# Order of the first loads and of the weight splitting in a two-layer attention kernel

## What is computed

```python
x = x + layer0(x, bias0, mask0, null_kv, ...)
x = x + layer1(x, mask1, null_kv, ...)
```

## Time and profile before

| | us |
|---|---|
| median of 3 runs | 2144.53 |
| lowest and highest | 2143.86, 2146.55 |
| the profiled execution, as timed | 2146.16 |
| its span in the profile | 2144.4 |
| TensorE busy | 2084.0 (97%) |
| VectorE, ScalarE, GpSimd busy | 1601.1, 1555.1, 1027.0 |

### The profile page before, as it was taken

The page is one execution under the profiler, slowest core; times in us unless marked ns, Lnnn a source line. Parts: engine busy times, 40 slices in busy tenths (PEclk is TensorE's granted clock), DMA queues, the critical chain, the costliest instruction groups (busy, mean ns, idle before and its releaser), DMA issues.

```text
span 2144.4 us, 72068 instructions
## 1 busy us (share of the span) xinstructions
PE 2084.0 (97%) x26363; PEld 1860.3 (87%) x26363; DVE 1601.1 (75%) x3422; ACT 1555.1 (73%) x6241; POOL 1027.0 (48%) x1510
## 2 busy tenths in 40 slices
PE   5899999999999999999999999999999999999987
PEld 4788988988988988988988988988988988988876
DVE  5877777777777777777777777777777777777765
ACT  3767777777777777777777777777777777777775
POOL 3445444445544444544544544544544544544543
PEclk8999999999999999999999999999999999999998
DMA  7212222222222212222222222222222212222211
GB/s 233 83 55 73 63 72 62 61 60 69 66 71 60 66 59 66 70 65 61 70 58 61 75 63 63 70 57 62 75 63 63 70 57 62 75 63 63 68 52 42
DMA packets 183034, 147.47 MB, mean 69 GB/s; under 512 B 121440, under 2 KB 125616, under 8 KB 182992
## 3 DMA queue, kind: packets, MB, share of 16 engines
q1 hardware_dynamic: 179008, 141.31, 22.3%
q10 hardware_dynamic: 3296, 4.46, 0.7%
q0 software_dynamic: 688, 1.14, 0.3%
HBM read 98.56 MB, written 37.77 MB: 64 GB/s over the span
## 4 chain that ended last, share of the span: by engine, by line
PE 92%; ACT 2%; SPq 2%; DVE 2%; issue 1%; POOL 1%; DMA 0%; POOLq 0%; DVEq 0%; ACTq 0%
PE psum L709 33%; PE psum L615 18%; PE psum L581 16%; PE psum L692 8%; PE psum L674 8%; PE psum L543 3%; PE psum L632 3%; PE psum L592 2%; SPq L386 1%; ACT o_hi L907 1%; ACT probs L901 1%; POOL probs L1479 0%; DMA xa<-in_x_dram 0%; DVE wo_lo L1188 0%; PE psum L623 0%
## 5 line engine op out<-in xcount | busy, mean ns | idle before, releaser
L901 ACT ACTIVATE probs<-probs,neg_max 128x129 f32<-128x129 f32 (+3 forms) x2048 | 712.3, 351 | 56.4 <-DVE neg_max L1144 56.3
L1469 POOL TENSOR_TENSOR masked_bias<-bias,pad_neg 128x516 f32<-128x516 f32 (+3 forms) x512 | 396.2, 806 | 211.8 <-DVE probs L1138 206.1
L1479 POOL TENSOR_TENSOR probs<-probs,den_inv 128x512 f32<-128x512 f32 (+3 forms) x512 | 369.4, 743 | 149.4 <-DVE den_inv L1149 149.4
L1491 POOL TENSOR_TENSOR y_out<-y_out,res 128x512 f32<-128x512 f32 x128 | 165.9, 1296 | 527.0 <-ACT y_out L865 527.0
L901 ACT ACTIVATION_READ_ACCUMULATOR probs<-probs,neg_max 128x1 f32 x2048 | 385.4, 188 | 0.0
L1154 DVE STREAM_TRANSPOSE probs_t<-probs 128x512 f32<-128x512 f32 (+3 forms) x512 | 229.9, 487 | 196.0 <-POOL probs L1479 194.9
L1138 DVE TENSOR_TENSOR probs<-psum,masked_bias 128x648 f32<-128x648 f32 x256 | 212.7, 831 | 114.3 <-PE psum L674 110.1
L709 PE MATMUL psum<-wo_hi,o_hi 128*128 128x512 f32 x1024 | 273.2, 409 | 8.2 <-ACT o_hi L907 7.5
L907 ACT ACTIVATE o_hi<-psum,null_v_col 128x512 fp32r<-128x512 f32 x256 | 162.1, 684 | 156.0 <-PE psum L692 156.0
L709 PE MATMUL psum<-wo_hi,o_lo 128*128 128x512 f32 x1024 | 262.5, 398 | 0.0
L709 PE MATMUL psum<-wo_lo,o_hi 128*128 128x512 f32 x1024 | 261.3, 397 | 0.0
(11 more groups left out here) (133 smaller groups left out, 3915.5 us busy)
## 6 DMA issues: line engine op xcount, KB each, us to landing
res<-in_x_dram SPq DMA_DIRECT2D x64, 256.0 KB, 2.7
v_rep<-v_kept SPq DMA_DIRECT2D x512, 32.0 KB, 1.8
x_of<-y_out SPq DMA_DIRECT2D x64, 256.0 KB, 2.1
res<-x_of SPq DMA_DIRECT2D x64, 256.0 KB, 2.7
out_dram<-y_out SPq DMA_DIRECT2D x64, 256.0 KB, 2.1
xa<-in_x_dram SPq DMA_DIRECT2D x63, 256.0 KB, 2.7
xa<-x_of SPq DMA_DIRECT2D x63, 256.0 KB, 2.7
q_aside<-qp SPq DMA_DIRECT2D x32, 256.0 KB, 3.1
```

The costliest lines, as they stand in the source:

```text
L901: x_ = nc.scalar.activation(s, s, ACT.Exp, bias=neg_max[:, b, n:n + 1], accum_out=den[:, b, n:n + 1])
L1469: m = nc.gpsimd.tensor_tensor(block(masked_bias, b), block(bias[u.layer], b), pad_neg[u.layer][:, 0:WIDTH[b]].unsqueeze(1).to_broadcast([P ...
L1479: m = nc.gpsimd.tensor_tensor(some, some, den_inv[:, b, :].unsqueeze(2).to_broadcast([P, 4, n]), ALU.mult)
```

## The change

- SyncE asks for the third input ahead of the bias loads, and for only 8 of the 16 bias loads; these have a semaphore of their own.
- GpSimd's queue asks for the other 8, behind w1, w2 and b2. GpSimd waits for both halves.
- ScalarE asks for weight pieces 4 to 7 after the first query halves are copied (before: ahead of the position network's first steps), and for 8 to 11 after the second halves, at the end of `begin`; the four high parts of pieces 4 to 7 all come behind that. `second0` gets one high part more, `first0` one fewer.
- Of the low parts of pieces 4 to 11, VectorE makes none in `begin` (before: one), four in `first0` (before: five) and four in `second0` (before: two). The statistics of the fourth input move from the start of `first0` to ahead of the first bias addition, and its normalising comes ahead of two of the row maxima.

```diff
--- before.py
+++ after.py
@@ -338,8 +338,9 @@
         sp_passed, dve_passed, pool_passed, pe_passed, act_passed = (
             sem(n) for n in ("sp_passed", "dve_passed", "pool_passed", "pe_passed", "act_passed"))
 
-        null_loaded, gain_loaded, null_row_loaded, null_v_loaded, g_out_loaded, rest_loaded, w1_loaded = (
-            sem(n) for n in ("null_loaded", "gain_loaded", "null_row_loaded", "null_v_loaded", "g_out_loaded", "rest_loaded", "w1_loaded"))
+        null_loaded, gain_loaded, null_row_loaded, null_v_loaded, g_out_loaded, w1_loaded = (
+            sem(n) for n in ("null_loaded", "gain_loaded", "null_row_loaded", "null_v_loaded", "g_out_loaded", "w1_loaded"))
+        rest_loaded = [sem(f"rest_loaded{n}") for n in range(2)]
         rows_loaded = [sem(f"rows_loaded{n}") for n in range(2)]
         raw_loaded = [sem(f"raw_loaded{n}") for n in range(4 * KC)]
         hi_done, lo_done = sem("hi_done"), sem("lo_done")
@@ -490,11 +491,10 @@
                 sp.dma_start(y_out[:, :], x[1]).then_inc(y_loaded, 16)
                 load_pieces(sp, range(KC))
                 start(sp, rows_loads[:3], rows_loaded[0])
-                start(sp, rest_loads[:8], rest_loaded)
+                load_xa(n)
+                start(sp, rest_loads[:8], rest_loaded[0])
                 for k in range(2):
                     sp.dma_start(keep[k][:, :], row((keep0, keep1)[k][0], S)).then_inc(keep_loaded[k], 16)
-                load_xa(n)
-                start(sp, rest_loads[8:], rest_loaded)
                 start(sp, rows_loads[3:], rows_loaded[1])
                 start(sp, [(null_v[:, :], row(null_kv[1], DH))], null_v_loaded)
                 load_res(w.even)
@@ -956,18 +956,17 @@
                 split_x(w.odd)
                 act.wait_ge(gain_loaded, 16 * len(gain_loads))
                 high_parts(range(KC))
-                load_pieces(act, range(KC, 2 * KC))
                 rstd_of_h(0)
                 sigmoid(0)
                 for k in range(2):
                     take_half(w, 0, k)
-                load_pieces(act, range(2 * KC, 3 * KC))
+                load_pieces(act, range(KC, 2 * KC))
                 null_norm()
-                high_parts((KC, KC + 1))
                 rstd_of_input(n)
                 for k in range(2):
                     take_half(w, 1, k)
-                high_parts((KC + 2, KC + 3))
+                load_pieces(act, range(2 * KC, 3 * KC))
+                high_parts(range(KC, 2 * KC))
 
             def first0(u, v, w, n, then):
                 rstd_of_input(w.odd)
@@ -980,14 +979,14 @@
                 take_half(w, 0, 0)
                 high_parts((2 * KC,))
                 take_half(w, 0, 1)
-                high_parts((2 * KC + 1, 2 * KC + 2))
+                high_parts((2 * KC + 1,))
                 act.wait_ge(null_loaded, 16 * len(null_loads))
                 split_o(u)
 
             def second0(u, v, w, n, then):
                 exponential(u, 0)
                 exponential(u, 1)
-                high_parts((2 * KC + 3,))
+                high_parts((2 * KC + 2, 2 * KC + 3))
                 copy_biases()
                 act.wait_ge(xn_done, w.odd.xdone)
                 take_y(v)
@@ -1283,36 +1282,34 @@
                 null_key_scaled()
                 input_statistics(n)
                 normalise(n)
-                low_parts((KC,))
                 second_layer()
                 dve.wait_ge(null_v_loaded, 16)
                 take_pair_v(w)
+                input_statistics(n2)
                 add_bias(then, 0)
 
             def first0(u, v, w, n, then):
-                input_statistics(w.odd)
                 add_bias(u, 1)
                 row_max(u, 3)
                 split_x(w.even)
+                normalise(w.odd)
                 row_max(u, 1)
-                normalise(w.odd)
                 row_max(u, 2)
                 row_max(u, 0)
                 normed(1)
                 inverse_sum(u, 0)
                 split_x(w.odd)
-                low_parts((KC + 1,))
+                low_parts((KC,))
                 turn(u, 0)
                 silu(1)
                 inverse_sum(u, 1)
+                low_parts((KC + 1,))
+                silu_transposed(1)
                 low_parts((KC + 2,))
-                silu_transposed(1)
-                low_parts((KC + 3,))
                 turn(u, 1)
                 last_layer()
-                low_parts((2 * KC,))
+                low_parts((KC + 3,))
                 diagonals_transposed()
-                low_parts((2 * KC + 1,))
                 add_bias(then, 0)
 
             def second0(u, v, w, n, then):
@@ -1325,11 +1322,12 @@
                 split_o(v, 1)
                 inverse_sum(u, 0)
                 dve.wait_ge(g_out_loaded, 16 * len(g_out_loads))
-                low_parts((2 * KC + 2,))
+                low_parts((2 * KC, 2 * KC + 1))
                 turn(u, 0)
                 centre_output(v)
                 inverse_sum(u, 1)
                 take_kvt(w)
+                low_parts((2 * KC + 2,))
                 turn(u, 1)
                 take_pair_v(w)
                 input_statistics(n)
@@ -1458,6 +1456,7 @@
 
             pool.wait_ge(raw_loaded[KC - 1], 32)
             start(pool, w1_loads, w1_loaded)
+            start(pool, rest_loads[8:], rest_loaded[1])
 
             def mask_bias(u):
                 wait(pool, keep_loaded[u.layer], u.sdone * 16)
@@ -1491,7 +1490,8 @@
                 nc.gpsimd.tensor_tensor(y_out[:, :], y_out[:, :], res[:, :], ALU.add).then_inc(out_done, 1)
 
             def begin(w, n, n2, then):
-                pool.wait_ge(rest_loaded, 16 * len(rest_loads))
+                for n_loaded in range(2):
+                    pool.wait_ge(rest_loaded[n_loaded], 16 * 8)
                 for b in range(BLOCKS):
                     square = block(bias[0], b)[:, :, 1 + b * R:]
                     nc.gpsimd.tensor_tensor(square, square, later[:, :].unsqueeze(1).to_broadcast([P, 4, R]),
```

## The result

The changed kernel takes 2165.86 us (median of 4 runs, 2164.94 to 2166.6) against 2145.54 before (2143.86 to 2147.49): a ratio of 1.0091, 95% interval 1.0079 to 1.0103. It is 20 us slower. The forecast was 2141.3 us with a range to 2146.5, so both the size and the side are wrong.

A forecast was written before the change was run, and what follows sets the result against it. TensorE bounds the kernel from 107.73 us on, so early gains shift the end one for one. The first addition 4.0 us sooner and 0.8 lost behind it make -3.2: 2144.5 - 3.2 = 2141.3 us, range 2136.4 to 2146.5.

The forecast's parts named there:

- GpSimd's half: Eight bias loads on GpSimd's queue behind w1, w2 and b2; forecast to land last, at 38.7 us.
- B: Moment the last bias load is there for GpSimd: 38.7 us forecast, 42.71 before; 26.65 + 2L for longer L.
- L: Landing time of GpSimd's loads beside ScalarE's weights: 5.8 us taken for w2, 6.3 for the last bias load.
- M: Start of VectorE's first addition of the masked bias: 44.3 us forecast, 4.0 sooner than 48.33.
- The copy of the keys: SyncE's request for this copy, forecast near 28 us instead of 42.08, costed at nothing.
- M minus B: From the last bias load's arrival to VectorE's first addition: 5.6 us, left as it is by the change.
- VectorE's floor for M: VectorE's readiness for the first addition after position product and fourth input's statistics: 40.8 us, the limit if bias comes sooner.
- From M to the steady part: First addition through `first0` and `second0`: 0.8 us lost together, bounds -0.6 and +2.
- The 0.8 won: Ahead of the second unit's additions, a VectorE low part of 1.40 us is gone: 0.8 us won, bounds 0 to 1.4.
- The third: Rival: GpSimd's loads starved behind ScalarE's weights; B 48.7, 2151.2 us at L = 11; chance 0.09.
- The second: Rival: the transfers on the shared engines were the limit; B stays at 42.7, 2145.3 us; chance 0.13.
- The chance of 0.08 for slower: Probability given to the whole kernel becoming slower by over 0.2%.

The follow-up runs named there:

- e6: The kernel before with only the bias loads cut into 32 of 32 partitions x 2 heads, all on SyncE's queue: 2143.01 us, ratio 0.9983.
- e8: The changed kernel with bias loads cut into 32 of 32 partitions x 2 heads, still split over both queues, and 2048 bytes of descriptor space: 2138.62 us.
- e9: e8 with the order of high and low parts in the first two units as before the change: 2137.39 us, ratio 0.9958.
- e10: e8 with only ScalarE's one high part moved back from `second0` to `first0`: 2137.30 us, ratio 0.9960.
- e5: The changed kernel with bias loads cut into 32 of 32 partitions x 2 heads, all asked for by SyncE: 2145.93 us, ratio 1.0000.
- e2: The changed kernel with the bias loads cut into 32 of 32 partitions x 2 heads, 16 on each queue: 2151.10 us, ratio 1.0024.
- e3: The changed kernel with the second eight bias loads back on SyncE's queue, old cut: 2148.12 us, ratio 1.0009.
- e4: The kernel before with only the second eight bias loads moved to GpSimd's queue: 2166.79 us, ratio 1.0089.
- e1: The changed kernel with GpSimd's descriptor space at 2048 bytes a partition instead of 1024: 2154.22 us, ratio 1.0034.
- e7: e6 with the third input asked for ahead of the bias loads: 2142.26 us, ratio 0.9980.
- e11: e6 with 2048 bytes of descriptor space: 2141.82 us, ratio 0.9984.

## Why the prediction was wrong

**The step that failed** is in GpSimd's half: "w2 (512) and b2 (128) leave room for one or two bias loads of 128 rows; the others wait until w2 has landed", and then 2.75 us for the rest. I counted rows. Two things were read off rightly: the queue holds a limited amount, and w2 waited for w1. The unit was wrong: the small loads of the start are spread over all engines, the bias loads over a quarter of them, so each takes as much space as w1. None follows b2, and no two are in flight. Nor was w2's landing the moment from which the others could go: w2 was there at 29.9, near the forecast, but the first bias load waited for b2, to 32.96. In place of B = 26.65 + 2L there are eight rounds, one behind the other: B is 63.8 us. Doubling the space (14.3 us of M back) and cutting the loads differently (15.7 us) show it from two sides.

The rows that could have warned were there: SyncE too needed 14.00 us for eight of these loads. I read that as the fault of the queue; e6 shows that the cut of the loads was part of it already before: there the first half of the bias takes 7.86 us.

**What held.** w1 landed at 22.7 (forecast 23.4), w2 at 29.9 (29.5). The copy of the keys went out at 28.07 (near 28). The third input was no wait. The first addition was released by GpSimd's masked bias. M minus B was 5.2 (5.6). VectorE's floor for M, 40.8, was nearly right: in e8 it was ready at 39.7.

**From M to the steady part** I had 0.8 us lost: 0.8 won ahead of the second unit, 1.6 lost in it. Measured: nothing won (19.62 against 19.57), 2.25 lost. The two places of the loss were right: 1.1 for the high part (1.2 forecast) and 1.1 for the low parts (0.4 forecast). The 0.8 won isn't seen between the two kernels; only e9 and e10, 19.98 and 18.66, show that low parts ahead of the second unit cost something.

**The rivals.** The third had the right side, and its condition (loads starved beside ScalarE's weights) was real: pauses of 8.6, 5.5 and 5.3 us while the weights ran, 1.9 to 2.8 when they were through. But its formula had two rounds; with eight even undisturbed loads lose. The second, that the shared engines are the limit, is out as the main cause, since the same bytes land by 34.5 in e5 and e8. The chance of 0.08 for slower was too small: I gave the slow side only to longer landings, and none to more rounds, though a queue that had just waited 9.77 us for one load was in the rows.

## What to carry to other kernels

Before loads are moved to GpSimd's queue, count what each needs there per engine, not in rows or bytes, and look whether its slowest dimension is a small one: four heads ahead of 32 rows made each load of 16 to 64 KB as bulky as one of 1 MB. Here a pause ahead of a request, with "issue" as its releaser, was the sign of a full queue, and the number of rounds multiplied the landing time. Look also at which loads share a semaphore: in these traces the space of w2 came back only with b2. The cut with 32 partitions outermost was asked for faster on SyncE's queue as well, above all beside ScalarE's weights (7.86 us for half of the bias instead of 14.00, and 7.80 instead of 14.64), a little also without them (7.85 instead of 8.80).

## What the runs showed of the hardware that was not expected

TensorE's clock made up for part of the loss. In the kernel before, a stall of 3.1 us ahead of 107.73 was followed by work at a lower granted clock (the column ahead of the DMA share and GB/s). The first two rows are the stretches, the third is the first work after the stall:

```profile
105.00:110.00 5.00, 2.27 (x37) 2.23 (x38) 3.97 (x6) 1.64 (x3) 2.00 (x2) 0.67 0.13 46
110.00:115.00 5.00, 5.00 (x16) 3.94 (x16) 4.45 (x9) 3.87 (x19) 3.25 (x4) 0.65 0.39 116
...
107.73 1.41 PE L674 MATMUL psum<-keys,q_t 64*64 64x129 f32 x32 [3.10 <-DVE wo_lo L1188]
```

0.67 and 0.65 are mixtures of 2.4 and 1.2 GHz. In the changed kernel the same work behind an equally long stall kept the full clock, and its first products took 0.82 us instead of 1.41:

```profile
125.00:130.00 5.00, 2.56 (x100) 1.86 (x97) 4.37 (x7) 3.29 (x7) 0.29 (x1) 1.00 0.25 64
130.00:135.00 5.00, 4.34 (x50) 3.74 (x51) 4.44 (x9) 2.77 (x12) 4.15 (x5) 1.00 0.37 109
...
130.66 0.82 PE L674 MATMUL psum<-keys,q_t 64*64 64x129 f32 x32 [3.10 <-DVE wo_lo L1187]
```

From the third unit's first addition to the second group of layer 1 projections behind it (6.36 us long in the chain of waits, at 128.75 before and 149.09 after) the changed kernel took 39.6 us and the one before 42.2. These 2.6 us are why a shift of M by 20.6 and a loss of 2.25 ended as 20.3 us at that point. The other traces fall into the same groups. Where the clock was low for some 7 us behind this stall (before, e2, e3, e4, e8, e10) the stretch took 42.15 to 42.43 us; where it was low for half as long (e1, e6, e7, e9, e11) 41.14 to 41.16; where it stayed full (the changed kernel and e5) 39.62 and 39.61. So this alone can make 1 to 2.6 us of difference between two profiles. What decides it wasn't tried; the stall's length doesn't: it is 3.1 to 3.2 us in all of them.

Two low parts beside GpSimd's division took 3.49 us instead of 2 x 1.40. The division took 3.81 us with two low parts beside it, 2.69 with one (before and e9), and 1.6 a unit later in e8, with none. Each was slower beside the other.
